# The last piece of layer 3 in two: 256 tokens of the last output block as 128 and 128

## The reference, cut to what matters

```python
out = jnp.einsum('btc,oc->bto', x, W_base) + b_base
h = jnp.einsum('btc,erc->bter', x, As)
lora = jnp.einsum('bter,eor,be->bto', h, Bs, w)
x = x + (out + lora * SCALING)
```

## Time and profile before

| what | us |
|---|---|
| median of 3 runs | 500.38 |
| lowest and highest run | 500.08, 500.94 |
| the profiled execution | 500.47 |
| its span | 498.4 |
| PE busy | 492.0 |
| DVE busy | 343.8 |
| ACT busy | 261.7 |

### The profile page before, as it was taken

How to read it: one execution, slowest core, us unless ns; L and a number is a source line. 1 busy time by engine, 2 the same in 40 slices (tenths; PEclk the granted TensorE clock), 3 DMA queues, 4 the chain that set the end, 5 groups by cost and what they waited for, 6 DMA issues and landing times.

```text
span 498.4 us, 6548 instructions
## 1 busy us (share of the span) xinstructions
PE 492.0 (99%) x2171; PEld 405.6 (81%) x2171; DVE 343.8 (69%) x603; ACT 261.7 (53%) x416; POOL 9.1 (2%) x14
## 2 busy tenths in 40 slices
PE   7999999999999999999999999999999999999997
PEld 5788788888888888888888888888888888888886
DVE  4868996877877677776766766566575666655655
ACT  6675463566656353555664445456554555444441
POOL 0510000000000000000000000000000000000000
PEclk9999999999999999999999999999999999999999
DMA  8914333333333343233333343232333233331002
GB/s 329 350 62 142 125 95 96 95 97 95 96 95 95 83 150 98 64 96 95 97 97 98 101 126 95 68 98 89 105 102 101 78 122 97 95 97 32 2 0 84
DMA packets 20336, 51.58 MB, mean 103 GB/s; under 512 B 2768, under 2 KB 3280, under 8 KB 20304
## 3 DMA queue, kind: packets, MB, share of 16 engines
q1 hardware_dynamic: 19872, 50.13, 32.2%
q10 hardware_dynamic: 432, 1.05, 0.5%
HBM read 49.07 MB, written 2.10 MB: 103 GB/s over the span
## 4 chain that ended last, share of the span: by engine, by line
PE 98%; DMA 1%; SPq 0%; issue 0%; DVE 0%
PE act_ps L288 10%; PE act_ps L289 10%; PE act_ps L290 10%; PE lin_ps L289 10%; PE lin_ps L288 10%; PE lin_ps L290 10%; PE acc_ps L288 10%; PE acc_ps L289 10%; PE acc_ps L290 10%; PE aux_ps L288 1%; PE aux_ps L290 1%; PE aux_ps L289 1%; DMA cols_w<-w_in 1%; PE acc_ps L357 1%; SPq L234 0%
## 5 line engine op out<-in xcount | busy, mean ns | idle before, releaser
L771 DVE TENSOR_TENSOR hid<-lin_ps,act 128x512 f32<-128x512 f32 x96 | 66.3, 691 | 98.5 <-PE lin_ps L290 98.3
L760 DVE TENSOR_TENSOR w_lo<-raw,w_hi 128x384 fp32r<-128x384 f32 (+1 forms) x221 | 122.5, 555 | 0.0
L487 ACT ACTIVATE hid_hi<-hid 128x512 fp32r<-128x512 f32 x112 | 70.8, 632 | 91.9 <-DVE hid L771 77.3
L481 ACT ACTIVATE act<-act_ps 128x512 f32<-128x512 f32 x96 | 57.3, 597 | 115.1 <-PE act_ps L290 115.1
L779 DVE TENSOR_TENSOR hid_lo<-hid,hid_hi 128x512 fp32r<-128x512 f32 x112 | 77.4, 691 | 26.0 <-ACT hid_hi L487 26.0
L467 ACT ACTIVATE w_hi<-raw 128x768 fp32r<-128x768 f32 x111 | 93.0, 838 | 0.0
L288 PE MATMUL act_ps<-x_hi,w_hi 128*128 128x512 f32 x228 | 88.6, 388 | 0.2 <-issue 0.2
L289 PE MATMUL act_ps<-x_lo,w_hi 128*128 128x512 f32 x228 | 88.5, 388 | 0.0
L290 PE MATMUL act_ps<-x_hi,w_lo 128*128 128x512 f32 x228 | 88.5, 388 | 0.0
L290 PE MATMUL lin_ps<-x_hi,w_lo 128*128 128x512 f32 (+1 forms) x226 | 87.7, 388 | 0.0
L289 PE MATMUL lin_ps<-x_lo,w_hi 128*128 128x512 f32 (+1 forms) x226 | 87.7, 388 | 0.0
(11 more groups left out here) (103 smaller groups left out, 325.0 us busy)
## 6 DMA issues: line engine op xcount, KB each, us to landing
raw<-w_in SPq DMA_DIRECT2D x112, 384.0 KB, 3.0
out<-x SPq DMA_DIRECT2D x7, 256.0 KB, 3.6
cols_w<-w_in SPq DMA_DIRECT2D x6, 256.0 KB, 6.5
x<-x_in SPq DMA_DIRECT2D x3, 512.0 KB, 6.3
x<-x_in ACTq DMA_DIRECT2D x1, 512.0 KB, 5.3
cols_w<-w_in SPq DMA_DIRECT2D x1, 288.0 KB, 3.2
mask<-mask_in ACTq DMA_DIRECT2D x1, 256.0 KB, 3.6
cols_w<-w_in ACTq DMA_DIRECT2D x1, 256.0 KB, 6.1
```

The lines of the kernel that those rows point to most:

```text
L481: act_e.activation(act[:, n % 2, :], act_ps[:, n % 2, :], func, bias=bias).then_inc(act_ready, 1)
L487: act_e.activation(hid_hi[:, n % 2, :], hid[:, n % 2, :], ACT.Copy).then_inc(hid_hi_ready, 1)
L760: ins = dve.tensor_tensor(w_lo[:, n % SPLIT, a:z], raw[:, n % RAW, a:z], w_hi[:, n % SPLIT, a:z].bitcast(F32), ALU.subtract)
L771: ins = dve.tensor_tensor(hid[:, n % 2, :], lin_ps[:, n % 2, :], act[:, n % 2, :], ALU.mult)
```

## The change

The last piece, 256 tokens, becomes two pieces of 128 tokens. The list has ten entries. The piece of tokens 256 to 383 stays in the second bank of `act_ps`, and the one of tokens 384 to 511 is made in the second bank of `lin_ps`. `layer3`, `add_l3`, `store` and the final wait follow the list and aren't edited.

```diff
             if b < B - 1:
                 return aux_ps[:, m, :]
-            return [act_ps[:, 0, :], lin_ps[:, 0, :] if t == 0 else act_ps[:, 1, :]][m]
+            if m == 0:
+                return act_ps[:, 0, :]
+            return {0: lin_ps[:, 0, :], T // 2: act_ps[:, 1, :], 3 * T // 4: lin_ps[:, 1, :]}[t]
 
         L3_PIECES = [(b, m, 0, T) for b in range(B) for m in range(CB)][:-1] + [
-            (B - 1, CB - 1, 0, T // 2), (B - 1, CB - 1, T // 2, T // 2)]
+            (B - 1, CB - 1, 0, T // 2), (B - 1, CB - 1, T // 2, T // 4), (B - 1, CB - 1, 3 * T // 4, T // 4)]
```

## The result

The changed kernel takes 0.17% longer than the kernel before: ratio 1.0017, 95% interval 1.0010 to 1.0024, which is 0.85 us (0.5 to 1.2) of 500.4. Medians of 22 runs each are 501.32 and 500.40 us. It lies within the 0.2% that was called no change. The forecast of +0.34 us had the sign right and under half of the size.

The account below looks back on a forecast made before the run. TensorE was taken as the bound, busy 492.0 of 498.4 us, with the change acting on the tail. Matmuls +0.62, add -0.13 and smaller last store -0.15 gave +0.34 us, a median of 500.7 us, range 500.1 to 501.3.

Parts of the forecast that it names:

- no change: Whole kernel: a difference within 0.2% (1.0 us), about what a measurement can tell from none; chance 0.91.
- The bound, and the place: Whole kernel: TensorE bounds it, chain 98% TensorE; everything the change touches lies after 494 us.
- The matmuls: Last 256 tokens: twelve 128-wide matmuls paced by weight loads, 0.115 us apart, end 0.62 us later.
- rival A: Last twelve matmuls: load hidden, 0.065 to 0.08 us each; 500.4, or 500.2 with quicker SyncE; chance 0.27.
- The adds: VectorE's tail: 0.352 us per 128-token add, first hidden, last ends 0.49 later; shorter add gives back 0.13.
- The stores: SyncE's tail: SyncE free, last issue 0.03 us after the add, engines idle before it, smaller last store saves 0.15.
- The sum for the tail: Tail: +0.62 for matmuls, -0.13 for the add, -0.15 for the smaller last store, +0.34 us in all.
- Completion (0.5) and the end (0.4) as before: nothing changes in them: After the last store's data: completion 0.5 and end 0.4 us unchanged, one more semaphore count at most.
- slower by over 0.2%: Whole kernel: the outcome of a slowdown beyond 0.2% (1.0 us), given a chance of 0.07.
- rivals B and C: Tail: B, load and matmul don't overlap, 502.1, chance 0.05; C, last store lands 1.9 us later, 502.6, chance 0.02.
- the lower end of the range: Whole kernel: 500.1 us, from rival A's -0.2 with a little of the runs' spread.

Follow-up runs that it names:

- pe_later: Kernel before plus three 256-wide matmuls behind the last, output unread: total moved by 0.3 us, interval holding zero; 5 of 11 runs had 2.52 to 2.96 us around the span.
- its repetition: The changed kernel run again with no edit, against the kernel before: ratio 1.0011 (1.0002 to 1.0019); 4 of 12 runs over 2.4 us around the span.
- one_store: Changed kernel's narrow matmuls and adds, but one 128 KB store for both last pieces, nine stores: longer time around the span in 7 of 11 runs.
- six_fewer: Changed kernel with 9 warm-up matmuls in place of 15: 11 of 12 runs over 2.5 us around the span.
- late_store: Changed kernel with its last 128 tokens stored as two of 64, eleven stores: 0.3% slower (1.0017 to 1.0042); 7 of 12 runs over 2.4 us around the span.
- those three kernels: Kernel before with six tiny matmuls after warm-up, or twelve wide ones behind the last; and last 256 tokens in four 64-token pieces. Second: span 499.1 to 500.5 us.

## Why the prediction was right, and short

- **The bound, and the place.** Right as far as a profile shows: TensorE leads the chain as before (97%, with 98% in the earlier trace rows), and the steps of the end are where the two profiles differ.
- **The matmuls.** The step that decided between forecast and rival A was right. 0.115 us from start to start was assumed, 0.112 measured, and the mean over the twelve is 0.107, as the first came for free. The last start is 1.18 us after the first, against 1.27 in the sum. Its length was taken as 0.28 less the columns, 0.23, and that was wrong: it is recorded at 0.28, since the narrow matmul waits for its weights within its length. The two errors nearly cancel, which is luck: TensorE ends 0.58 later in the tail, 0.62 was forecast. The Trainium skill's 107 ns for the load of 128 columns ("TensorE: Matmul & The Clock Gate", "LDWEIGHTS (loading the stationary operand)") agrees with the measured 0.112 us. Its 81 ns per pair at 128 wide (the same page, "Back-to-back issue gap"), which rival A stood for, isn't what these loads allow: 112 ns at 192, 128 and 64 wide.
- **The adds.** 0.35 us each as worked out; the add ends 1.84 us after the first matmul, against 1.40, so +0.44 where the sum had +0.49. The first add is hidden as forecast.
- **The stores.** SyncE wasn't a bound, the last issue came 0.03 after the add, the engines idled for 0.3 us before its packets, and it landed in 1.6 in place of 1.8: -0.2 where -0.15 was forecast.
- **The sum for the tail.** +0.24 us against +0.34.
- **"Completion (0.5) and the end (0.4) as before: nothing changes in them".** This is the step that failed, and the reason why the sum was short. It took the way from the last landing to the end, and what lies around the span, as one fixed amount, 0.09 above the median and no term. In 14 of 22 runs it is 0.6 to 1.1 us over the 1.94 of before. The 0.07 given to "slower by over 0.2%" is what rivals B and C had together, and neither was a case for it. That the effect came to stand just under that line, at 0.17%, and the median at the top of the range, 501.32 against 501.3, is luck: the term that carries most of it wasn't in the sum.
- **Rivals B and C.** Neither: 0.112 is far under 0.175 us, and no store of the changed kernel's tail took over 2.1 us to land.
- **A sum in rival A.** A last issue at 496.27 gives data until 496.27 + 0.83 + 0.32 = 497.42, which is 0.08 us before the 497.50 of before and not 0.2. At 0.35 per issue its own terms put the issue at 496.18 and the gain at 0.17, so the lower end of the range stands.

**What stays open.** Shown: the extra time around the span comes with TensorE ending 0.36 us later in the tail (pe_later, with nothing else altered) or 0.58 (the changed kernel, its repetition, one_store, six_fewer and late_store). In the five runs of experiments with such an end it is there in 34 of 58 executions. It doesn't need the tenth store, the narrow adds or a longer program. Not shown is the mechanism. It isn't simply that TensorE leaves last, since ends 1.4 and 1.9 us later show none of it. The traces point at the fetch of TensorE's program. Where its 18th packet falls inside the span, a store's issue is held up by about 1 us, and none of the 35 executions of those three kernels has over 2.4 us around the span. In the one profile with over 2.4 the packet comes after the end. A loss of the same size that falls now here, now there would fit both, but one such profile doesn't show it, and no run was made that moves the packet alone.

## What to carry to other kernels

When each matmul brings its own weight load of 128 columns, don't cut its moving side below the width whose streaming covers that load (256 did, 192 didn't): a piece at the end that is smaller saves in the add and the store, and loses it on TensorE. Before splitting a last store, see whether the DMA engines ever run dry ahead of it; they had been full until 0.1 us before, so there was almost nothing to win. And a sum made from the span alone leaves out what lies around it: list total minus span run by run for both kernels, as that can move while every profile stays the same.

## What was not expected of the hardware

- The time around the span has two levels, 1.74 to 2.12 and 2.48 to 3.12 us, and an end of TensorE 0.36 us later, in work that nothing waits for, moves 5 of 11 runs to the upper one.
- The issue of a store in SyncE's queue, 0.33 to 0.46 us otherwise, took 1.23, 1.38 and 1.49 us once each in three of the profiles, each time while a 16 KB packet of TensorE's program was moving, and ended 0.37 to 0.39 us after it.
- The recorded length of a matmul doesn't shrink below 0.27 to 0.28 us at 192, 128 or 64 columns, when it waits for its weights; only the first of a narrow series, with its weights ready, shows 0.25, 0.22 and 0.20.
